# Fusion kernel: first stage in token tiles of 98, 98 and 77, with the four attention weights multiplied together in pairs

## The reference, cut to what matters

```python
h = concat(patches @ W.T, txt)             # 196 + 77 = 273 tokens x 256
xn = layernorm(h)
q, k, v = xn @ Wq, xn @ Wk, xn @ Wv        # all 256 x 256
s = where(causal, q @ k.T, -inf)           # 273 x 273
a = softmax(s * 256 ** -0.5) @ v
h1 = h + a @ Wo
x0 = layernorm(h1)                         # and max |x0| over everything
```

## Time and profile before

| what | value |
|---|---|
| median of 3 runs | 5960.48 us (5957.14 to 5983.22) |
| the profiled execution, its own time | 5973.35 us |
| its span | 5971.3 us |
| granted TensorE clock, mean over the span | 0.854 |
| PE busy over the span | 4632.2 us (78%) |
| DVE, ACT, POOL busy over the span | 64%, 42%, 10% |
| first matmul of `phase_a`, and its last store issued | 46.2 us, 839.1 us |

### The profile page before, as it was taken

How to read it: one execution, slowest core, us unless ns; L and a number is a source line. 1 busy time by engine, 2 the same in 40 slices (tenths; PEclk the granted TensorE clock), 3 DMA queues, 4 the chain that set the end, 5 groups by cost and what they waited for, 6 DMA issues and landing times. The chain is left out here.

```text
span 5971.3 us, 101861 instructions
## 1 busy us (share of the span) xinstructions
PE 4632.2 (78%) x27583; PEld 3020.9 (51%) x27583; DVE 3844.7 (64%) x9327; ACT 2507.9 (42%) x5760; POOL 597.5 (10%) x928
## 2 busy tenths in 40 slices
PE   6999978850029888587787786777799899789888
PEld 5667657640015555355555554555455555444444
DVE  3444433348878878777777665555677777477776
ACT  1222224347533333377777774222366666400000
POOL 0000000000000000100000000111111111122221
PEclk9999989975569989777777777888799999899999
DMA  2111113348974444332222222555433333211110
GB/s 65 52 54 52 50 53 144 144 169 253 355 274 125 127 130 123 87 75 69 69 69 69 71 72 69 157 154 154 105 93 85 88 94 91 77 45 46 49 50 27
DMA packets 379998, 617.03 MB, mean 103 GB/s; under 512 B 43190, under 2 KB 310004, under 8 KB 379892
## 3 DMA queue, kind: packets, MB, share of 16 engines
q1 hardware_dynamic: 367572, 614.35, 35.1%
q0 software_dynamic: 12320, 1.40, 0.2%
HBM read 345.02 MB, written 269.21 MB: 103 GB/s over the span
## 5 line engine op out<-in xcount | busy, mean ns | idle before, releaser
L1645 DVE TENSOR_REDUCE e_neg<-ps 91x1 f32<-91x273 f32 x1536 | 571.9, 427 | 137.4 <-PE ps L1466 130.0
L1578 ACT ACTIVATE e_probT<-ps 91x273 f32<-91x273 f32 x1536 | 491.7, 393 | 292.9 <-PE ps L1466 292.2
L1193 PE MATMUL ps<-k_downT,f_o 128*91 128x256 f32 x1152 | 260.1, 385 | 453.6 <-DVE f_o L1101 453.4
L2320 PE MATMUL ps<-m_we,m_xT 128*128 128x512 f32 x1104 | 521.6, 621 | 0.0
L1193 PEld LDWEIGHTS ps<-k_downT,f_o 128*91 128x91 f32 x1152 | 183.0, 161 | 522.4 <-issue 454.6
L1464 PE MATMUL ps<-c_mask_kq,c_identb 91*91 91x91 bf16 x1536 | 325.8, 243 | 104.4 <-ACT g_probT L1578 79.4
L1466 PE MATMUL ps<-e_k,e_q 96*91 96x273 bf16 x1536 | 344.0, 307 | 64.9 <-DMA e_k<-s_parts 28.8
L2254 DVE SCALAR_TENSOR_TENSOR m_acc<-ps,m_weight,m_acc 128x256 f32<-128x256 f32 x552 | 261.7, 481 | 173.6 <-PE ps L2320 163.7
L1466 PE MATMUL ps<-g_q,g_k 102*91 102x273 bf16 (+5 forms) x1536 | 331.0, 296 | 49.1 <-DVEq L1651 48.5
L2320 PEld LDWEIGHTS ps<-m_we,m_xT 128*128 128x128 f32 x1104 | 211.4, 198 | 223.3 <-issue 208.9
L1466 PE MATMUL ps<-e_q,e_k 128*91 128x273 bf16 x1536 | 286.7, 291 | 38.3 <-DMA e_q<-e_shift 36.4
(11 more groups left out here) (303 smaller groups left out, 10057.6 us busy)
## 6 DMA issues: line engine op xcount, KB each, us to landing
s_gate<-b_gu SPq DMA_DIRECT2D x32, 819.0 KB
s_up<-b_gu SPq DMA_DIRECT2D x32, 819.0 KB
c_g<-s_gate SPq DMA_DIRECT2D x32, 819.0 KB, 7.0
s_gated<-c_g SPq DMA_DIRECT2D x32, 819.0 KB
d_g<-s_gated SPq DMA_DIRECT2D x32, 819.0 KB, 10.4
d_u<-s_up SPq DMA_DIRECT2D x32, 819.0 KB
s_o<-d_o SPq DMA_DIRECT2D x32, 819.0 KB
f_o<-s_o SPq DMA_DIRECT2D x32, 819.0 KB
```

The lines of the kernel that those rows point to most:

```text
L1193: last = nc.tensor.matmul(ps[0:R, t // 2, (t % 2) * D:(t % 2 + 1) * D], o[:, u, k, t * R:(t + 1) * R], downT[:, k, :], start=(k == 0), sto ...
L1578: nc.scalar.activation(probT[0:R, p % 8, b, :], src, ACT.Exp, scale=float(HD) ** 0.5 if kinds[h] == COS else 1.0)\
L1645: last = nc.vector.tensor_reduce(neg[:, u, t, h:h + 1], src, AX.X, ALU.max, negate=True)
L2320: last = nc.tensor.matmul(ps[0:R, EBANK[m % 4], :], xT[:, u, k, t * R:(t + 1) * R], we[:, k, 2 * p:2 * p + 2, :].rearrange("p e d -> p (e ...
```

## The change

The tokens of `phase_a` stand in tiles of 98, 98 and 77 rows (A_ROWS): two tiles of patches, and one of text alone. The embedding so has two tiles. Before the loop PE multiplies the weights in pairs, Wqk = Wq Wk^T and Wvo = Wv Wo, and ACT copies both out of PSUM. The scores are (xn Wqk) xn^T, with xT itself as the moving operand; the values are xn Wvo, and `attend` gives the output of the attention at once, with the transposed probabilities as the stationary operand. `copy_a` and `project` are gone, as are one of the two halves of `copy_qk` and the second copy in `copy_tok`. The order of the stages is new on PE, ACT and DVE, and so are the PSUM banks: turned x and values in 0 and 1, the mixed x and the turned probabilities in 2 and 3, scores and outputs in 4 and 5, embedding and turned x0 in 6 and 7. The store of h1 is two transfers. The 21 rows below the text tile are filled once by DVE, and the first text loads wait for it. The loads at the start are ordered anew. On the host Wq, Wk and Wv are handed over transposed. The diff, cut:

```diff
+RA = PATCHES // 2
+A_ROWS = (RA, RA, TEXT)
+A_FIRST = (0, RA, 2 * RA)
...
+        TURNED, MIXED, SCORED, EXTRA = 0, 2, 4, 6
+        causal = {0: (SCORED, 2 * RA), 1: (SCORED, 0), 2: (SCORED + 1, 0)}
+        PT = {0: (0, 0), 1: (1, 0), 2: (1, T - RA)}
...
@@ SP: store_h1 is two transfers; the loads at the start
-            for u in range(2):
-                load_patches((0, u), u)
-                load_text((0, u), u)
-            for w, dram in ((wq, wq_dram), (wk, wk_dram), (wv, wv_dram), (wo, wo_dram)):
+            load_patches((0, 0), 0)
+            for w, dram in ((wqT, wq_dram), (wkT, wk_dram), (wvT, wv_dram), (wo, wo_dram)):
                 sp.dma_start(w[:], dram.rearrange("(k p) n -> p k n", p=128)).then_inc(w_loaded, 16)
+            sp.wait_ge(padded, 4)
+            load_text((0, 0), 0)
+            load_patches((0, 1), 1)
+            load_text((0, 1), 1)
...
@@ ACT
+            for j, to in enumerate((wqk, wvo)):
+                act.wait_ge(folding, j + 1)
+                nc.scalar.copy(to[:], ps[:, 2 * j:2 * j + 2, 0:D]).then_inc(folded, 1)
...
-                nc.scalar.copy(h[0:P_LAST, u, 2, :], ps[0:P_LAST, 1, 0:D]).then_inc(S["tok_out"].sem, 1)
...
-            def copy_a(n, u, i):
...
-            pipeline(act, NB, ((copy_x, 0), (copy_v, 0), (exponentials, 0), (copy_tok, 1), (copy_x0, -1),
-                               (copy_a, 0)))
+            pipeline(act, NB, ((copy_x, 0), (copy_tok, 1), (exponentials, 0), (copy_v, 0), (copy_x0, -1)))
...
@@ DVE
+            nc.vector.memset(h[64:RA, :, NT - 1, :], 0.0).then_inc(padded, 1)
+            nc.vector.memset(h1[64:RA, :, NT - 1, :], 0.0).then_inc(padded, 1)
+            nc.vector.memset(mx[:], 0.0).then_inc(padded, 1)
+            nc.vector.memset(den[:], 1.0).then_inc(padded, 1)
...
-                for j, to in enumerate((qT, kT)):
-                    dve.wait_ge(S["qk"].sem, S["qk"].at(n, j + 1))
-                    nc.vector.tensor_copy(to[:, u], ps[:, 4 + 2 * j:6 + 2 * j, 0:T]).then_inc(S["qk_out"].sem, 1)
+                dve.wait_ge(S["g"].sem, S["g"].at(n))
+                nc.vector.tensor_copy(gT[:, u], ps[:, MIXED:MIXED + 2, 0:T]).then_inc(S["g_out"].sem, 1)
...
-            pipeline(dve, NB, ((residual, -1), (copy_qk, 0), (normalise_h1, -1), (maxima, 0), (maximum, -1),
-                               (copy_p, 0), (statistics, 1), (normalise_h, 1)))
+            pipeline(dve, NB, ((residual, -1), (normalise_h1, -1), (copy_g, 0), (maximum, -1), (statistics, 1),
+                               (maxima, 0), (normalise_h, 1), (copy_p, 0)))
...
@@ PE: embed_first and embed_second are one tile each, into bank EXTRA
+            def embed_first(n, u, i):
                 pe.wait_ge(patches_loaded[u], 16 * (i + 1))
                 pe.wait_ge(S["tok_out"].sem, S["tok_out"].at((n[0], n[1] - 1)))
+                pe.wait_ge(S["x0T_out"].sem, S["x0T_out"].at((n[0], n[1] - 3)))
+                embed(u, 0)
...
+            def mix(n, u, i):
                 pe.wait_ge(S["xT_out"].sem, S["xT_out"].at(n))
+                pe.wait_ge(S["pT_out"].sem, S["pT_out"].at((n[0], n[1] - 1)))
+                for m in range(CT):
+                    for k in range(CT):
+                        last = nc.tensor.matmul(ps[:, MIXED + m, 0:T], wqk[:, k, m * 128:(m + 1) * 128],
+                                                xT[:, u, k, :], start=(k == 0), stop=(k == CT - 1))
+                last.then_inc(S["g"].sem, 1)
...
@@ scores: waits for g_out and for h1 of the element before
+                        last = nc.tensor.matmul(ps[0:rows, bank, col:col + w], gT[:, u, k, A_FIRST[t]:w],
+                                                xT[:, u, k, 0:w], start=(k == 0), stop=(k == CT - 1))
...
@@ turn_x0
+                pe.wait_ge(S["x0T_out"].sem, S["x0T_out"].at((n[0], n[1] - 1)))
+                if following(n, NB):
+                    pe.wait_ge(S["tok_out"].sem, S["tok_out"].at((n[0], n[1] + 2)))
...
@@ attend
+                for t in range(NT):
+                    for k in range(t + 1):
+                        bank, col = PT[k]
+                        q0 = col + A_FIRST[t] - A_FIRST[k]
+                        last = nc.tensor.matmul(ps[0:A_ROWS[t], SCORED + t // 2, (t % 2) * D:(t % 2 + 1) * D],
+                                                probT[0:A_ROWS[k], u, bank, q0:q0 + A_ROWS[t]],
+                                                v[0:A_ROWS[k], u, k, :], start=(k == 0), stop=(k == t))
+                last.then_inc(S["y"].sem, 1)
+
+            pe.wait_ge(w_loaded, 16 * 4)
+            for j, (left, right) in enumerate(((wqT, wkT), (wvT, wo))):
                 for m in range(CT):
                     for k in range(CT):
+                        last = nc.tensor.matmul(ps[:, 2 * j + m, 0:D], left[:, k, m * 128:(m + 1) * 128], right[:, k, :],
                                                 start=(k == 0), stop=(k == CT - 1))
+                last.then_inc(folding, 1)
+            pe.wait_ge(tok_loaded, 16)
+            pe.wait_ge(folded, 2)
+            pipeline(pe, NB, ((turn_x, 0), (embed_first, 1), (mix, 0), (embed_second, 1), (scores, 0), (values, 0),
+                              (turn_p, 0), (turn_x0, -1), (attend, 0)))
```

More of the change, by code:

```diff
@@ L170, in phase_a @@
+        w_loaded, tok_loaded, folding, folded, padded = (sem(k) for k in ("w_loaded", "tok_loaded", "folding",
+                                                                          "folded", "padded"))
         patches_loaded = [sem(f"patches_loaded{u}") for u in range(2)]
@@ L269, in exponentials @@
                     bank, col = causal[t]
-                    w = (t + 1) * R
-                    nc.scalar.activation(prob[:, u, t, 0:w], ps[0:R, bank, col:col + w], ACT.Exp,
-                                         bias=nb[:, u, t:t + 1], scale=scale,
-                                         accum_out=den[:, u, t:t + 1]).then_inc(S["p"].sem, 1)
-            def copy_a(n, u, i):
-                act.wait_ge(S["a"].sem, S["a"].at(n))
-                act.wait_ge(S["y"].sem, S["y"].before(n))
-                nc.scalar.copy(aT[:, u], ps[:, 2:4, 0:T]).then_inc(S["a_out"].sem, 1)
+                    rows, w = A_ROWS[t], end(t)
+                    nc.scalar.activation(prob[0:rows, u, t, 0:w], ps[0:rows, bank, col:col + w], ACT.Exp,
+                                         bias=nb[0:rows, u, t:t + 1], scale=scale,
+                                         accum_out=den[0:rows, u, t:t + 1]).then_inc(S["p"].sem, 1)
             def copy_x0(n, u, i):
@@ L316, in maxima @@
                     bank, col = causal[t]
-                    nc.vector.reduce_max(mx[:, u, t:t + 1], ps[0:R, bank, col:col + (t + 1) * R], AX.X)\
+                    rows = A_ROWS[t]
+                    nc.vector.reduce_max(mx[0:rows, u, t:t + 1], ps[0:rows, bank, col:col + end(t)], AX.X)\
                         .then_inc(S["mx"].sem, 1)
@@ L365, in _, with turn_rows @@
                 S[k].give(pe)
-            pe.wait_ge(w_loaded, 16 * 5)
-            def patch_tile(n, u, t):
-                m = R if t < NT - 1 else P_LAST
+            def turn_rows(x, bank):
+                for ct in range(CT):
+                    for t in range(NT):
+                        rows = A_ROWS[t]
+                        last = nc.tensor.transpose(ps[:, bank + ct, A_FIRST[t]:end(t)],
+                                                   x[0:rows, t, ct * 128:(ct + 1) * 128], c["ident"][0:rows, 0:rows])
+                return last
@@ L438, in attend @@
                 pe.wait_ge(S["pT_out"].sem, S["pT_out"].at(n))
-                for m in range(CT):
-                    for k in range(NT):
-                        moving = probT[:, u, 0, :] if k == 0 else \
-                            probT[:, u, 1, (k - 1) * 2 * R:(k - 1) * 2 * R + (NT - k) * R]
-                        last = nc.tensor.matmul(ps[:, 2 + m, k * R:T], v[:, u, k, m * 128:(m + 1) * 128],
-                                                moving, start=(k == 0), stop=(k == NT - 1))
@@ L445, in attend @@
-                last.then_inc(S["a"].sem, 1)
-            def project(n, u, i):
-                pe.wait_ge(S["a_out"].sem, S["a_out"].at(n))
-                for t in range(NT):
+                for t in range(NT):
+                    for k in range(t + 1):
+                        bank, col = PT[k]
+                        q0 = col + A_FIRST[t] - A_FIRST[k]
+                        last = nc.tensor.matmul(ps[0:A_ROWS[t], SCORED + t // 2, (t % 2) * D:(t % 2 + 1) * D],
+                                                probT[0:A_ROWS[k], u, bank, q0:q0 + A_ROWS[t]],
+                                                v[0:A_ROWS[k], u, k, :], start=(k == 0), stop=(k == t))
@@ L453, in project @@
                                                 start=(k == 0), stop=(k == CT - 1))
-                last.then_inc(S["y"].sem, 1)
-            pipeline(pe, NB, ((turn_x, 0), (patches_first, 1), (queries_and_keys, 0), (values, 0), (scores, 0),
```

(3 more changed lines are left out.)

162 lines of the change are left out of this document (74 added, 88 removed).

## The result

The changed kernel takes 5747.04 us (median of 4 runs, 5725.51 to 5764.31) against 5971.85 us of the kernel before (4 runs, 5957.14 to 5989.06): a ratio of 0.9621, 95% interval 0.9575 to 0.9666. The forecast was 5736 us in a range of 5698 to 5782. The profiled execution took 5748.39 us, forecast 5749; its span went from 5971.3 to 5746.7, by 224.6 us for 224.2 forecast. The 11 us between 5736 and the median measured are another matter: the median of the kernel before was 5971.85 in this comparison, and the forecast had started from 5960.5.

The account below looks back on a forecast made before the run. PE was taken to bound the first stage, a new turn being 15.95 us of work plus 1.0 of waits. 747.35 - 31 x 16.95 - 1.6 + 3.9 = 224.2 us off 5960.5 gave 5736 us, range 5698 to 5782.

Parts of the forecast that it names:

- The bound: First stage's loop: PE busy 95.32 of 100 us sets the turn, so removed PE work is gained one for one.
- PE work of a turn: First stage's loop: PE work per turn falls by 8.14 us, from 24.09 to 15.95.
- The waits: PE's waits in a new turn: 1.0 us, from 0.39 before `turn_p` and 0.60 before `attend`.
- 16.95 and 1.6: A new turn takes 16.95 us; the first turn, starting at half clock, costs 1.6 more.
- The chain: DVE and ACT work from residual to copied probabilities in six steps, letting the next turn start at 16.94 us.
- the tie of step 2: DVE ends the next element's statistics at 9.9 us of the turn, just as the scores are seen; maxima follow.
- forecast's 8.14 us a turn: First stage's loop: the new PE work of 15.95 us is this much less than the old turn.
- Start and end: First stage outside the loop: start changes by nothing, 2 us to either side; end falls from 30.9 to 27.0 us.
- the 4.4 added for a lowered clock: Last turn of the first stage: 4.4 us on top of 22.6 at full clock; ends nothing and 7.4.
- The rival that ends slower: First stage's loop: two PE pauses a turn bring the granted clock to 1.2 GHz; 32.9 us a turn, 6233 us; chance 0.02.
- a rival with 0.02, as a whole cause: Transfers set the turn, or later stages with the same code give the gain back: 5960 us; chance 0.02.

Follow-up runs that it names:

- the two runs with tiles changed alone: Kernel before with token tiles of 98, 98, 77: 5895.6 us; changed kernel with tiles put back to 91, 91, 91: 5825.8 us.
- the run with the maxima first: Changed kernel with DVE's maxima ahead of the next element's statistics and the normalising behind the copy of the turned probabilities: 5739.4 us (2 runs).
- tiles alone: Kernel before with only its token tiles changed to 98, 98, 77, the h1 store in two transfers: 5895.6 us, ratio 0.9859.
- tiles and products, order of before: Changed kernel's arithmetic, tiles and banks, with the stages of PE, ACT and DVE in the kernel before's order: 5770.9 us, ratio 0.9644.
- with the next x ahead of attend: Changed kernel with the next element's x transposes put before `attend` on PE, and `copy_x` last on ACT: 5729.8 us (5 runs).
- the kernel before with more increments: Kernel before with 24 more semaphore increments on each of ACT, PE and DVE ahead of the first stage's loop: 5982.8 us, ratio 1.0007.
- half the embedding: Changed kernel with three of the six input slices of the patch embedding not multiplied: a turn of 15.52 us.
- more increments on ACT and on PE: Two runs of the changed kernel with 24 more semaphore increments ahead of the first stage's loop: on ACT 5747.9 us, on PE 5756.6 us.
- the values first: Changed kernel with `values` ahead of `scores` on PE, no work added: 5903.5 us, ratio 0.9871.
- the three runs above: 24 semaphore increments added on the changed kernel's ACT (5747.9 us) or PE (5756.6), or on the kernel before's ACT, PE and DVE (5982.8).

## Why the prediction was right, point by point

**The bound.** Right. PE set the turn before and after; the two runs with tiles changed alone show it from both sides (2.77 and 2.57 us for 2.7 of work).

**PE work of a turn.** Right to 0.02: 16.57 less its 0.62 of waits is 15.95, as forecast, and every stage is within 0.05 of its term. The tile of 14 rows did cost as much as one of 91. The waits are the mis-sized term here: I took 1.0, and they are 0.62 in one turn of a pass and 0.79 in the other. From the row of the last maximum to the first exponential I took 0.40, and in the turn shown it is 0.23 (323.70 less 323.47); from `copy_p` to `attend` I took 0.15, and it is 0.05. Neither price is new. The two turns of a pass differ in the first of these hand-overs in both kernels, in the second in the old loop, and I had taken the dearer value of each from different turns. The other turn of the old loop has 0.23 for the first (628.16 less 627.93):

```profile
627.49 0.44 DVE L317 TENSOR_REDUCE a_mx<-ps 91x1 f32<-91x273 f32 x1 [0.50 <-PE ps L416]
628.16 0.33 ACT L271 ACTIVATE a_prob<-ps,a_nb 91x91 f32<-91x91 f32 x1 [1.85 <-DVE a_nb L321]
```

and the changed kernel's other turn has 0.40 (340.44 less 340.04):

```profile
339.20 0.84 DVE L329 TENSOR_REDUCE a_mx<-ps 98x1 f32<-98x98 f32 x3
340.44 0.34 ACT L285 ACTIVATE a_prob<-ps,a_nb 98x98 f32<-98x98 f32 x1 [2.92 <-DVE a_nb L333]
```

No turn of the old loop had both 0.40 and 0.15: the sum of the two hand-overs there is 0.38 in one turn and 0.46 in the other, where I took 0.55. The 0.17 us between 0.40 and 0.23 is also what the two turns of the changed kernel differ by. The first turn, with the start's half clock, took the 18.57 us that 16.95 and 1.6 come to; the other thirty took 16.65 in the mean. So the gain in 31 turns was 229.3 us (747.35 less 518.10) where 220.3 was forecast.

**The chain.** Right in each of its steps and in the tie of step 2: the statistics ended at 10.06 us of the turn and held the maxima, which the run with the maxima first confirmed with 0.21 us a turn. The pause before `attend`, forecast 0.60, is 0.50. By single steps from the kernel before, in us a turn:

| kernel | turn | step |
|---|---|---|
| before | 24.11 | |
| tiles alone | 21.33 | -2.77 |
| tiles and products, order of before | 17.70 | -3.63 |
| the changed kernel | 16.71 | -0.99 |
| with the next x ahead of attend | 16.16 | -0.55 |

Of the forecast's 8.14 us a turn not all was work: 1.4 were the two old waits and what goes with them (0.60 ahead of `attend` and 0.78 ahead of `project`). The products remove 4.05 us of PE work, 1.85 of queries and keys and 2.20 of the old `attend` (2.98 less 0.78). They bring 3.63 in the old order, because the waits grow: from 1.3 us a turn with tiles alone to 1.7. The largest of them, the 1.05 before the transposes of x, is not there with tiles alone, where `project` and the wait before it stand at that place. The new order brings another 1.0, more than half of these waits.

**Start and end.** The start came out at nothing, as forecast (60.91 for 60.87). The end is mis-sized: 579.01 to 601.36 is 22.35 us where I had 27.0. The chain without cover was worked out as 22.6; what failed is the 4.4 added for a lowered clock. The rows of the end:

```profile
585.03 0.41 PE L434 MATMUL ps<-a_xT,a_gT 128*98 128x98 f32 x2 [2.56 <-DVE a_gT L322]
587.28 2.75 PE L422 MATMUL ps<-a_wvo,a_xT 128*98 128x256 f32 x12
591.41 2.81 PE L467 MATMUL ps<-a_v,a_probT 98*98 98x256 f32 x12 [0.43 <-DVE a_probT L338]
601.36 0.39 SPq L223 DMA_DIRECT2D s_x<-a_x0T  x1
```

After a pause of 2.56 us the values and `attend` ran at full speed, 2.81 for 12 records, where the old end had 5.43 for 2.83 in `project`. That loss was not a property of the old end either. In the trace of the kernel before with more increments the end has the same pauses, but `attend` and `project` ran at full speed, and it took 26.85 us for 30.9. Of each trace, the first row is the long pause; the kernel before is first:

```profile
820.25 0.72 PE L429 MATMUL ps<-c_ident,a_prob 91*91 91x91 f32 x6 [2.04 <-ACT a_prob L271]
826.58 5.43 PE L451 MATMUL ps<-a_wo,a_aT 128*91 128x256 f32 x12 [0.70 <-ACT a_aT L278]
```

```profile
825.54 0.72 PE L434 MATMUL ps<-c_ident,a_prob 91*91 91x91 f32 x6 [2.05 <-ACT a_prob L272]
830.07 2.83 PE L456 MATMUL ps<-a_wo,a_aT 128*91 128x256 f32 x12 [0.70 <-ACT a_aT L279]
```

So some 4 of the 8.6 us gained at the end, and of the 237.8 of the stage, are half clock that this one trace of the old kernel had and the other had not. The forecast's lower end for this term, nothing, is what came. As the same end can lose the clock in one trace and not in another, that is in part luck.

**The clock.** The rival that ends slower was priced at 6233 us, with two short pauses as its cause. In the changed kernel it did not come. By the Trainium skill (TensorE: Matmul & The Clock Gate, A second HAM failure mode: psum-queue depth-cycling) a PE that idles briefly and often has a clock that goes back and forth; this case agrees for its longer pauses alone. The 6233 us, with all of the work at half clock, was the far end of that. Pauses of 0.1 to 0.3 and of 0.5 a turn, and one of 1.05 to 1.4 in the runs with the old order and with half the embedding, left it at 1.00; one of 2.07 or 2.24, with another of 0.34 behind 1 us of transposes, brought it to 0.91, with 1.2 GHz in part of each `attend`. But the length of a pause is not all that counts. At the end of the stage the pause of 2.56 left the clock alone in four traces of this stage (the changed kernel twice, and with more increments on ACT and on PE). In the run with the maxima first, the same pause had the scores behind it start at half clock, and the end took 23.82 us for 22.35:

```profile
579.65 0.65 PE L434 MATMUL ps<-a_xT,a_gT 128*98 128x98 f32 x2 [2.57 <-DVE a_gT L322]
```

And in the last turn with the old order, `mix`, behind pauses of 0.91 and 0.70, took 3.58 us for 2.01. What decides it was not tried.

**What the sum did not have.** From the last store of the first stage to the end of the span it was 5132.2 us before and 5145.3 after (5971.3 - 839.12 and 5746.7 - 601.36). So the first stage gained 237.8 us, 13.6 more than forecast, and 13.2 were given back in stages whose code is the same. I had that only as a rival with 0.02, as a whole cause. Over thirteen traces, the time from the first load of `phase_b` to the end lies between 5114.0 (half the embedding) and 5141.6 (more on PE), and traces whose work is the same differ as much: 5120.4 with more on ACT and 5141.6 with more on PE, against 5133.6 and 5137.5 of the changed kernel, and 5120.7 and 5129.7 for the kernel before without and with more increments. So 13 us is within what these stages do by themselves. Most of that is in the last stage: 805.2 and 805.8 in the changed kernel's traces, 797.1 with more on ACT, 793.8 before, 781.3 with the tiles alone, 783.0 with half the embedding. The granted clock of that stage goes with it: 0.91 in the changed kernel, 0.92 with more on ACT, 0.93 before, 0.94 in the two shortest. The whole times can't settle how much is given back: the 11 executions of the kernel before and the 8 of the changed one that belong to the result and to its repeat differ by 231.5 us in the mean, with a standard error of 7.

About 6 us are not scatter: `phase_b` took 453.8 to 455.0 us in the ten traces with the products of weights, and 447.1 to 448.4 in the three without. Of the groups of instructions in `phase_b`, before and after, one has changed:

```profile
L661 PE MATMUL ps<-b_x,k_gateT 128*128 128x273 f32 x768 | 207.7, 432 | 69.6 <-DVE b_x L638 69.6
```

```profile
L686 PE MATMUL ps<-b_x,k_gateT 128*128 128x273 f32 x768 | 212.2, 439 | 70.9 <-DVE b_x L663 70.9
```

The first is the kernel before, the second the changed one; the columns are busy us and mean ns of one, then the idle time ahead of it. The group that follows PE's pause in each turn is 4.5 us busier and its pauses are 1.3 longer, while the group after it has 182.2 in both. So PE runs longer at half clock behind its pauses. Why it does so only behind this first stage stays open. It is not a shift of the code by 24 instructions (the three runs above), not the tiles or the two transfers of h1 (tiles alone has 447.5), and not the time at which `phase_b` starts (764.1 us with tiles alone and 764.5 with the values first, with 447.5 and 455.0). The new PSUM banks and scratch tiles, which all ten share, were not tried apart from the products.

## What to carry to other kernels

Price a tile of PE work by its moving columns: 14 rows of output cost as much as 98, so tiles that divide the data evenly save a whole pass. When removed work was also the cover of a chain on other engines, redo the order of the stages with the change, and walk the chain once with start-to-start times from the trace; it gave every pause in the loop here to 0.3 us. Take the hand-overs from one and the same turn, and look at both turns of a pass. And look for the pause that is as long as some stage of the next element.

## What the runs showed of the hardware

Order alone can cost clock. Without a single added instruction, a pause of 2.07 us in each turn, with a short one of 0.34 soon after it, put some eight of the twelve records behind them at 1.2 GHz (4.36 us from start to start for 2.67). In all it cost 151 us in the stage. The pauses are less than half of that (31 x 2.0 = 62); for the rest, the granted clock of 0.86 over the 669 us from 60.9 to 730 gives an estimate (0.14 x 669 = 94). In the loop of the run with the old order, a pause of 1.05 a turn left it at 2.4 GHz.

The same pauses do not always cost the same: at the end of the stage the kernel before lost 4 us to half clock in one trace and nothing in another, whose loop was the same.

Twenty-four semaphore increments on PE took 3.7 us more in front of its next matmul, 0.15 us each.
